# Mixing two chunks of x on quarters of the array, two blocks at a time

## What is computed

```python
def _L0_cond_ref(x, condition, weights):
    W = weights[condition]                      # one 32x32 matrix for each batch
    return jnp.einsum('bct,bcd->bdt', x, W)     # "mixing" of the 32 rows of a batch

q, k, v = hidden @ Wq + bq, hidden @ Wk + bk, hidden @ Wv + bv      # 512 -> 4096
q, k = rms_norm(q, gq), rms_norm(k, gk)
attn = softmax(q k^T * scale); out = (attn v) @ Wo + bo             # 32 heads of 128, 32 tokens each
x = x + out
x = x + ffn(cond2(x))                           # quantised weights with a low-rank update, 8 low-rank experts
```

## Time and profile before

| what | value |
|---|---|
| median of 3 runs | 1451.32 us (1451.01 to 1451.55) |
| the profiled execution | 1450.27 us |
| its span, first to last instruction | 1448.4 us |
| PE busy | 1443.8 us (100% of the span), 14507 matmuls |
| PEld busy | 1200.6 us (83%) |
| DVE busy | 1079.1 us (75%) |
| ACT busy | 726.7 us (50%) |
| POOL busy | 746.3 us (52%) |
| granted TensorE clock | 1.0 |

### The profile page before, as it was taken

How to read it: one execution, slowest core, us unless ns; L and a number is a source line. 1 busy time by engine, 2 the same in 40 slices (tenths; PEclk the granted TensorE clock), 3 DMA queues, 4 the chain that set the end, 5 groups by cost and what they waited for, 6 DMA issues and landing times.

```text
span 1448.4 us, 34721 instructions
## 1 busy us (share of the span) xinstructions
PE 1443.8 (100%) x14507; PEld 1200.6 (83%) x14507; DVE 1079.1 (75%) x1507; ACT 726.7 (50%) x1331; POOL 746.3 (52%) x530
## 2 busy tenths in 40 slices
PE   9999999999999999999999999999999999999999
PEld 8788888888888888888888888888888888888887
DVE  8788868687786777875478888867987667667663
ACT  7766676766766667676333333334432322222221
POOL 7668777777777877776345555514561111112100
PEclk9999999999999999999999999999999999999999
DMA  4211011110111011102443343447653334244230
GB/s 152 66 45 45 31 38 45 45 44 25 45 45 45 29 39 45 45 31 67 138 155 137 131 136 134 145 151 244 200 195 110 103 118 132 85 136 132 74 118 30
DMA packets 106989, 135.13 MB, mean 93 GB/s; under 512 B 6224, under 2 KB 89424, under 8 KB 106320
## 3 DMA queue, kind: packets, MB, share of 16 engines
q1 hardware_dynamic: 105968, 132.49, 27.7%
q10 hardware_dynamic: 864, 0.42, 0.1%
HBM read 86.75 MB, written 46.14 MB: 92 GB/s over the span
## 4 chain that ended last, share of the span: by engine, by line
PE 97%; DVE 1%; ACT 1%; DMA 0%; issue 0%; SPq 0%; DVEq 0%
PE bank L717 42%; PE bank L960 25%; PE bank L736 21%; PE bank L919 4%; PE bank L845 3%; PE bank L988 1%; PE bank L1006 1%; DMA qk<-in_x_nat 0%; PE bank L666 0%; DVE qreg L1708 0%; PE bank L1017 0%; PE bank L974 0%; ACT xs_hi L1160 0%; DVE wa L1624 0%; DVE sqst L1708 0%
## 5 line engine op out<-in xcount | busy, mean ns | idle before, releaser
L717 PE MATMUL bank<-xs_hi,wa 128*128 128x512 f32 x1792 | 563.3, 392 | 0.1
L1527 POOL TENSOR_TENSOR accr<-accr,sqst 128x512 f32<-128x512 f32 x248 | 353.2, 1435 | 147.7 <-ACT sqst L1197 107.5
L717 PEld LDWEIGHTS bank<-xs_hi,wa 128*128 128x128 f32 x1792 | 336.3, 188 | 74.1 <-DVE qk L1775 2.3
L717 PE MATMUL bank<-xs_lo,wa 128*128 128x512 f32 x896 | 348.7, 389 | 0.0
L960 PE MATMUL bank<-ot,wo_main 128*128 128x512 f32 x1344 | 316.4, 392 | 0.0
L960 PEld LDWEIGHTS bank<-ot,wo_main 128*128 128x128 f32 x1344 | 249.5, 188 | 52.6
L736 PE MATMUL bank<-wv,xs_hi 128*128 128x512 f32 (+1 forms) x1008 | 282.6, 366 | 0.1
L1624 DVE TENSOR_TENSOR wa<-wraw,wa 128x256 fp32r<-128x256 f32 (+1 forms) x160 | 157.0, 982 | 96.7 <-ACT wa L1106 95.0
L1322 ACT ACTIVATE ot<-bank,vec 128x256 fp32r<-128x256 f32 x256 | 100.3, 476 | 239.0 <-PE bank L960 146.6
L736 PEld LDWEIGHTS bank<-wv,xs_hi 128*128 128x128 f32 x1008 | 182.1, 189 | 32.9 <-issue 1.9
L717 PEld LDWEIGHTS bank<-xs_lo,wa 128*128 128x128 f32 x896 | 168.3, 188 | 33.2
(11 more groups left out here) (224 smaller groups left out, 1726.9 us busy)
## 6 DMA issues: line engine op xcount, KB each, us to landing
values_b<-v_spill SPq DMA_DIRECT2D x60, 512.0 KB, 4.9
wraw<-in_wqk SPq DMA_DIRECT2D x32, 512.0 KB, 3.5
v_spill<-qk SPq DMA_DIRECT2D x64, 256.0 KB, 2.3
v_spill<-sqst SPq DMA_DIRECT2D x64, 256.0 KB, 2.2
score_spill<-sqst SPq DMA_DIRECT2D x32, 256.0 KB, 2.0
wraw<-in_wv SPq DMA_DIRECT2D x16, 512.0 KB, 5.1
wraw<-score_spill SPq DMA_DIRECT2D x16, 512.0 KB, 4.0
spare<-in_wo SPq DMA_DIRECT2D x15, 512.0 KB, 4.8
```

The costliest lines, as they stand in the source:

```text
L717: ins = pe.matmul(dst[:, :], wa[:, col:col + P], xpart[:, j - 1, kt, n * CH:(n + 1) * CH], start=(first and k == 0), stop=(k == 5), skip_g ...
L1527: pool.tensor_tensor(a, a, sq_slot(count), ALU.add).then_inc(acc_done, 1)
```

## The change

`mix_chunk` now makes its blocks in pairs (g = 0 and g = 1 of the same r). Since the matrix is block-diagonal, rows 0 to 63 of a tile only reach columns 0 to 63, and rows 64 to 127 only columns 64 to 127. Each tile of a block is made of four matmuls of 64 rows, 64 features and 64 columns. First the upper half of the rows of one block with the lower half of the other, for four tiles; then a wait of PE on its own semaphore `mix_crossed`; then the halves crossed. Both blocks of a pair are complete only at the pair's end. `mix_group` still uses full matmuls.

```diff
+        mix_crossed = sem("mix_crossed")
...
+            crossed = [0]
+
+            def mix_tile(block, half, t):
+
+                g, r, c, i = block
+                rows = slice(half * 64, (half + 1) * 64)
+                for d in range(2):
+                    ins = pe.matmul(mix_bank(g, r)[d * 64:(d + 1) * 64, t * P + half * 64:t * P + (half + 1) * 64],
+                                    x_in[c][rows, t, i * P + d * 64:i * P + (d + 1) * 64],
+                                    mixw[rows, c * TC + t, rows], start=True, stop=True)
+                return ins
+
+            def mix_pair(one, other):
+
+                for t in range(TC):
+                    mix_tile(one, 0, t)
+                    ins = mix_tile(other, 1, t)
+                ins.then_inc(mix_crossed, 1)
+                crossed[0] += 1
+                pe.wait_ge(mix_crossed, crossed[0])
+                for t in range(TC):
+                    first = mix_tile(one, 1, t)
+                    second = mix_tile(other, 0, t)
+                first.then_inc(mixed, 1)
+                second.then_inc(mixed, 1)
+
...
-                for i in range(KI):
-                    mix_block_of(i % 2, (0, 3)[i // 2] if c == 0 else (1, 2)[i // 2], c, i)
+                for i in (0, 2):
+                    r = (0, 3)[i // 2] if c == 0 else (1, 2)[i // 2]
+                    mix_pair((0, r, c, i), (1, r, c, i + 1))
```

## The result

| what | before | changed |
|---|---|---|
| median of 6 runs each, on one chip | 1451.15 us | 1458.26 us |
| lowest to highest | 1450.19 to 1451.55 | 1455.36 to 1460.34 |
| ratio | | 1.0047 (95%: 1.0037 to 1.0058) |
| the profiled execution, its span | 1450.27, 1448.4 | 1457.52, 1455.7 |

The changed kernel is slower by 7.1 us. That lies outside the range of the prediction, on the other side of the old time.

A forecast was written before the change was run, and what follows sets the result against it. PE, busy for the whole span, was taken to bound the kernel; p1(2) starting 0.45 us earlier gave 1451.32 - 0.45 = 1450.9 us, with a range of 1450.0 to 1452.6.

The forecast's parts named there:

- The new mixing: Step on the mixing: 64 quarter rows at 0.0149 us plus a 0.30 us self-wait, 1.25 us a pair instead of 1.79.
- quarters go less well: Rival in the mixing: only two quarters run together, 0.030 us a row, 2.21 us a pair, 1453.5 us; no separate chance given.
- no overlap: Rival in the mixing: quarters don't overlap, 0.056 us a row, 7.2 us slower, 1458.5 us; chance 0.03.
- The 25 ns between starts: Rule against the change: matmul starts never closer than about 25 ns, a pair 1.6 us plus wait, some 1452.5 us.
- Where the saving goes: Step from the mixing to p1(0): of 2.2 us saved on PE's own work, 0.5 us is left.
- PE has issued the last pair by 9.49 + 2.50 = 12.0: Step at the mixing's end: PE is done issuing by 12.0 us, then idles 1.5 us before p1(0) at 13.5.
- The sum: Final step: p1(2), at 37.22 us, comes 0.45 us earlier, so the median becomes 1451.32 - 0.45 = 1450.9 us.
- The chain (0,1), ACT, DVE: Path from mixed block (0,1) through ACT and DVE to p1(0): block at ACT 0.56 us earlier, p1(0) at 13.5, not 14.00.
- more is gained: Rival after p1(0): PE's waits at 26.89 and 37.22 us vanish too, 0.45 + 0.5 us, 1450.3 us; chance 0.08.
- the clock: Rival after the mixing: TensorE's clock falls to its lower level, costing 1.7 to 2.9 us, 1452.6 to 1453.8 us; chance 0.08.
- A shift that changes after p1(2), which my argument excludes: Sign of being wrong: everything behind p1(2) was to shift by the same 0.45 us.

The follow-up runs named there:

- only0_lean: Kernel before with chunk 0 alone on quarters and the eight unused small matmuls ahead of it left out: 1449.79 us, ratio 0.9996.
- only0: Kernel before with quarters for chunk 0 alone, chunk 2 with full matmuls: 1450.44 us, ratio 0.9999.
- Experiments 8 to 10: Useless small matmuls ahead of some heads' scores: 128 or 256 more instructions in the kernel before (1453.54, 1452.71 us), 128 more in the changed kernel (1454.99 us).
- experiments 3 to 5: Kernel before with 96 more small matmuls ahead of the mixing (1463.11 us), or PE held before chunk 2 until chunk 3 (1459.37 us) or chunk 1 (1456.28 us) landed.
- hold: Kernel before, full matmuls, with PE held ahead of chunk 2 until chunk 3 has landed: one run, 1459.37 us.
- hold1: Kernel before, full matmuls, with PE held ahead of chunk 2 until chunk 1 has landed: one run, 1456.28 us.
- late_x: Changed kernel with SP issuing chunks 1 and 3 of x only after four blocks are mixed: 1457.85 us, ratio 1.0051.
- halves: Changed kernel with one matmul of 64 rows and 128 columns in place of two quarters: 1456.27 us, ratio 1.0032.

## Why the prediction was wrong

**The new mixing: right.** Rate and self-wait came out as taken: rounds of four quarters every 0.058 us, 0.0146 a row (0.0149 forecast). The last matmul ahead of the first self-wait was issued at 7.51 and the next load came at 7.80: 0.29 us (0.30 forecast). A pair takes 1.27 us (1.25). The order of the quarters, which no row showed, made no difference, so the rivals "quarters go less well" and "no overlap" fell. The 25 ns between starts, which I had weighed and put aside, are dealt with below.

**Where the saving goes: wrong, by the step "PE has issued the last pair by 9.49 + 2.50 = 12.0".** The third pair did start at 9.54. But I counted PE's work in time only. The table of the change says that sixteen full matmuls became 64; 48 more in a chunk, each two matmuls and two weight loads in the trace, so 192 more instructions a chunk, in a stretch where PE takes them faster than ever. What an engine can run is bounded by what has been brought to it. Of that the trace of before had signs: the queue q8, x's loads on all the DMA engines until 15 us, and waits of PE "for issue" of up to 0.4 us in each head's scores. I read none of them as a supply. Had I counted, the forecast would have been open, since no row that I had shows how far PE can run ahead (in the trace of before no packet starts with more than 297 records left ahead of its piece); but the rival would have been there: an instruction packet of before starts at 11.31, and the new mixing wanted its instructions at 10.0.

**The sum: wrong in its first term.** Instead of -0.45, p1(2) moved by +3.67. No run had both chunks on quarters without the stop, so this sum itself was never measured. The chain (0,1), ACT, DVE shows in `only0_lean`: ACT takes (0,1) at 10.23 (before 11.60), DVE's low part of the weights runs from 11.57 to 12.68, p1(0) starts at 12.74 and p1(2) moves by -1.13; of this 0.46 is a mixing that starts earlier (6.37 instead of 6.83). That `only0` comes out at -0.57 is luck as far as the forecast goes: its p1(0) is 0.10 late behind the short stop, and the gain is made by PE's waits after p1(0), which I had let stand and put into the rival "more is gained".

**The rival "the clock": right in kind, wrong in cause and size.** I let it fall for the 1.5 us of idle time that my own chain gave, at 0.08. It fell, for an idle time of 3.25 us that had another cause. It cost about 1.05 us between p1(0) and mix_group(2), plus what the second half of the mixing lost: pairs three and four had some 2.0 us of work left at the stop, and took 3.7.

**"A shift that changes after p1(2), which my argument excludes": the argument was wrong.** It held that what is unchanged in order and content keeps its time. The shift grew from 3.7 to 7.3 us behind p1(2), 1.9 of it by one stop caused by nothing but the number of instructions ahead of it. Experiments 8 to 10 show this cause; the experiments 3 to 5 show that of the first stop and of the clock.

**What stays open.** The first packet starts at 9.8 to 11.6 us in all the programs, even where the loads came later; what it waits for I can't say. Of the 0.90 us between 64 and 113 us, 0.36 come in one step that is a third stop of the same kind: PE goes on with the piece behind record 1729 (449 + 5 x 256) at 77.33 us, 2.36 after its packet's start. Another 0.27 come in a step at 113 us that `hold` and `hold1` have too, with the count of before. The remaining 0.27 and the 0.76 in small steps after 113 us are measured, not explained. Nor did any run show why the clock fell in `late_x` after 1.89 us of idle time and held in `halves` after 3.01, or why it stays low for 3.4 us in some executions and for 6.8 in others. Whether the spread of the changed kernel's runs (1455.36 to 1460.34) comes from that was not tried.

## What to carry to other kernels

Count an engine's instructions beside its time. Where a change makes four short instructions out of one, above all in the first microseconds while data loads fill the DMA queues, look whether the engine can be supplied: a wait "for issue" in the middle of a group, where the program has no wait, is the sign. A change of the count also moves the ends of the pieces in all of the program behind it, and a dense burst of short instructions may then stop for 2 to 3 us hundreds of microseconds away; so read the whole trace before a difference is put down to the place of the edit, and try the same edit with some instructions more.

## What the runs showed of the hardware

- PE's instructions come in pieces of 256 records, packets of 16384 bytes on q8. The stops told of above all came after record 449 + k x 256, in ten programs of this study, and PE went on 2.3 to 2.7 us after the packet's start. No packet started with more than 299 records left ahead of its piece, in fourteen traces. A packet itself takes about 1.0 to 1.1 us (medians of the traces).
- In bursts of short instructions a piece runs out: the 96 last rows of a head's scores and their loads pass in a microsecond, and where a piece ended in their last rows the stop was 1.9 to 3.0 us.
- Quarters of 64x64 run at 0.058 us for four; halves of 64 rows with 128 columns at 0.112 us for two, no better than full matmuls. What sets the pace here goes with the 128 columns of the weights, not with the 64 moving ones. The Trainium skill's page "TensorE: Matmul & The Clock Gate" (section "Wait — 56ns, not 53.3ns?") has matmul starts never closer than about 25 ns; rows of quarters start on average 15 ns apart, so the measurement decides against it here.
- PE waiting for its own semaphore took 0.29 us from the issue of the last matmul to the next weight load.
- Idle time alone can cost the clock. With 3.44 us of it (`hold1`, one run) the granted clock was 0.5 for 3.4 us, with 6.61 us (`hold`, one run) for 6.8 us, in a kernel that otherwise holds 1.0 to its end.
